# A decoder layer with routed experts: row buffers twice, reciprocals spread by transfers, another order of the sequence stage

## The chip, the cores and the metric

The kernel runs on one core of a Trainium2 chip. The core has five engines with their own instruction queues, each of which works strictly in order: TensorE (PE; its weight loads are shown as PEld), VectorE (DVE), ScalarE (ACT), GpSimd (POOL) and SyncE (SP), which here only issues transfers. They wait for each other through semaphores. The metric is the device time of one execution in microseconds, from the first to the last instruction with what the launch puts around it; the median of several runs counts. The profile and the trace come from one further execution.

## What is computed

A post-norm decoder layer on 16 sequences of 256 tokens, 256 features, all in float32:

```python
# attention 1 (one head): scores q.k, an elementwise function of them, softmax, values, output
theta = BASE_THETA + K_DOP * sigmoid(qk) + K_NOR * tanh(qk) + K_SERO * relu(qk)
attn = softmax(theta, axis=-1)
out = einsum('bst,btd->bsd', attn, v) @ Wo.T + bo
# attention 2 (cross): 16 heads of 16 features, in blocks of 64 tokens, keys and values from ctx
scores = einsum('bnqhd,bnkhd->bnhqk', qh, kh) / sqrt(hd)
out = einsum('bnhqk,bnkhd->bnqhd', softmax(scores), vh) @ out_proj_w.T + out_proj_b
# feed-forward: 32 experts of width 128, 4 chosen per token within 2 of 4 groups, and a shared one
x = layernorm(x + attn1(x)); x = layernorm(x + attn2(x, ctx)); x = layernorm(x + ffn(x))
```

## The kernel before

**Stages.** After a short setup (products of the weights of attention 1, constants), the sequence stage takes the 16 sequences through both attentions, the shared expert and the routing. It scatters each token's row to the four experts chosen, into the DRAM tensor `routed`. Then 159 expert blocks of 128 rows gather from `routed`, and an output stage adds up and normalises.

**The sequence stage is a pipeline written by hand.** On each engine a loop `for t in range(nseq + 5)` names its steps in a fixed order; a step `f(e, t - k)` works for the sequence that is k steps behind. So in step t the engines work on several sequences at once: attention 1 on sequence t, cross attention on t - 1, gates, router and shared expert on t - 3, the shared output and the scatters on t - 4. Nothing else sets the order: each engine does its list from top to bottom, and a wait of one entry holds all that stands behind it. PE starts its step t with `pe_scores2(t - 1)` (L410). The names used below, in PE's order: cross scores `pe_scores2` L410, `pe_x2T` (transposes, L274, as all transposes), `pe_z` L314, `pe_vo` L326, scores 1 `pe_scores1` L335, `pe_shared_out` L541, `pe_router` L507, `pe_gate` L518, `pe_pTa` (transposes of `sha`), `pe_k` L371, `pe_prT` (transposes of the softmax `pr`), `pe_pTb` (of `shb`), `pe_av1` L354, `pe_up` L529, `pe_av2` L464, `pe_den` L447, `pe_v` L381, `pe_rank` L550, `pe_x1T`, `pe_spread` L477, `pe_q` L393, `pe_out2` L487.

**Passes of many small products.** Four passes of PE consist of 32 or 64 products on parts of the array: the cross scores, `pe_av2`, `pe_den` and `pe_spread`. `pe_den` sums the exponentials into one bank (128 rows x 64), DVE's `vec_rden` takes the reciprocals (L1096), and `pe_spread` multiplies them with a 0/1 matrix so that every output dimension has its own reciprocal. ACT copies the product with the values to `num` (`act_num`), and `vec_o` (L1102) multiplies the two:

```python
                            m = e.matmul(bank[7][32 * j:32 * j + 32, at], c("spread")[:, dims:dims + 32], rden[i % 2][:, :],
                                         start=True, stop=True)
```

**Buffers.** The 8 PSUM banks are shared by all passes, which the `after(...)` waits keep apart. `x1`, `kM`, `vM`, `row` and `idx` exist once.

**POOL** adds the constant to the residuals (`pool_xc`, `pool_xc2`), takes the inverse roots of the layer norms (`pool_rs1`, `pool_rs2`), copies each token's row four times into `row` (`pool_row`, L1382) and issues 8 indirect scatters per sequence (L1398, L1405), which wait for the cross scores of the same step. `pool_row` waits until the scatters of the sequence before have landed. DVE's `vec_key` (last operation L1201) gives the rows their places and weights.

**SP** issues in each step `load_xT`, `load_x`, `load_c` (the inputs of the sequence, single buffers), `store_acc`, and `load_rest`, a 768 KB share of the expert weights. `load_rest(0)` first fills a part of `routed` with zeros (`zrow`, 4 MB).

## Time and profile before

| | us |
|---|---|
| median of 3 runs | 878.8 |
| lowest and highest | 878.05, 879.95 |
| the profiled execution | 873.4 |
| its span, first to last instruction | 871.2 |

The profiled execution is 0.6% shorter than the median; the span leaves out 2.2 us around the instructions. The profile has a page of busy times and strips over 40 slices of the span, and the trace behind it answers with timelines of an engine, transfers with their time to landing, and busy times by stretch. Times are microseconds from the start of the span. "L410" is a line of the kernel. The end of a PE row is modelled, so a pass is read from its own start to the start of the next. The count behind a PE row is twice that of the products, since each float32 product is two records.

### The profile page before, as it was taken

How to read it: one execution, taken by the hardware profiler on the slowest of the kernel's cores; microseconds unless marked ns; L12 is line 12 of the kernel's file. 1: busy time of each engine (PE TensorE's matmuls, PEld its weight loads, DVE VectorE, ACT ScalarE, POOL GpSimd, SP SyncE). 2: the span in 40 equal slices, each digit the busy share in tenths (PEclk: the TensorE clock that was granted, in tenths of full speed). 3: DMA queues.
4: the chain of work that ended last, by engine and by line, in shares of the span. 5: the costliest groups of instructions: out<-in, count | busy, mean ns of one | idle time of the engine just before them, and what ended most of it. 6: DMA issues, size and time to landing. Idle time of an engine off the chain costs nothing.

```text
span 871.2 us, 23658 instructions
## 1 busy us (share of the span) xinstructions
PE 801.1 (92%) x7881; PEld 658.8 (76%) x7881; DVE 546.1 (63%) x2115; ACT 461.5 (53%) x1150; POOL 408.3 (47%) x501
## 2 busy tenths in 40 slices
PE   7778999999999999999999555899999999999885
PEld 6567788888888888888887444688888888887332
DVE  2244577887788787887788852355555555554366
ACT  1455566655665666655665111466666666665133
POOL 0200235464455546464545662455656555556123
PEclk9999999999999999999999875999999999999999
DMA  6472223243324322342331124855555555552996
GB/s 222 125 174 79 80 69 103 100 136 93 121 76 142 106 103 82 133 124 94 104 127 58 67 86 134 301 163 166 165 162 159 169 165 158 161 170 91 327 401 242
DMA packets 69654, 125.06 MB, mean 144 GB/s; under 512 B 9665, under 2 KB 43329, under 8 KB 69282
## 3 DMA queue, kind: packets, MB, share of 16 engines
q1 hardware_dynamic: 51394, 81.60, 30.3%
q0 software_dynamic: 13776, 37.77, 12.1%
q10 hardware_dynamic: 4368, 4.20, 1.4%
q8 instruction: 67, 1.10, 0.5%
q14 instruction: 49, 0.40, 0.2%
HBM read 73.16 MB, written 50.36 MB: 142 GB/s over the span
## 4 chain that ended last, share of the span: by engine, by line
PE 78%; DMA 6%; POOL 5%; issue 4%; SPq 4%; ACT 2%; DVE 1%; ACTq 0%; POOLq 0%; DVEq 0%
PE banks L584 15%; PE banks L274 11%; PE banks L597 7%; PE banks L393 4%; SPq L623 4%; PE banks L381 3%; PE banks L354 3%; PE banks L314 3%; PE banks L335 3%; PE banks L371 3%; PE banks L326 3%; PE banks L487 3%; PE banks L518 3%; PE banks L541 3%; PE banks L529 3%
## 5 line engine op out<-in xcount | busy, mean ns | idle before, releaser
L1431 POOL DMA_INDIRECT y<-yb_tile,idcol_tile x159 | 153.0, 962 | 123.6 <-ACT yb_tile L948 121.3
L584 PE MATMUL banks<-w_expert_tile,xbT_tile 128*128 x636 | 166.4, 385 | 3.9 <-ACT xbT_tile L786 3.9
L584 PEld LDWEIGHTS banks<-w_expert_tile,xbT_tile 128*128 128x128 f32 x636 | 109.9, 193 | 13.5 <-issue 4.9
L1259 DVE COPY hbT_tile<-banks 128x128 f32<-128x128 f32 x159 | 46.4, 292 | 117.2 <-PE banks L274 117.2
L1398 POOL DMA_INDIRECT routed<-row_tile,idx_tile x64 | 63.3, 989 | 85.0 <-PE banks L410 66.5
L948 ACT ACTIVATE yb_tile<-banks,rowsb_tile 128x256 f32<-128x256 f32 x159 | 75.4, 474 | 48.8 <-PE banks L597 41.5
L597 PE MATMUL banks<-w_expert_tile,hbT_tile 128*128 x318 | 95.7, 383 | 0.0
L1366 POOL TENSOR_TENSOR rs_tile<-ve_tile,half_neg_tile 128x2 f32<-128x2 f32 x16 | 11.5, 717 | 140.6 <-DVE ve_tile L1046 140.6
L1405 POOL DMA_INDIRECT routed<-row_tile,idx_tile x64 | 65.7, 1027 | 17.7 <-issue 17.7
L942 ACT ACTIVATE gb_tile<-banks 128x128 f32<-128x128 f32 x159 | 44.2, 278 | 55.5 <-PE banks L584 55.5
L786 ACT ACTIVATE xbT_tile<-banks 128x256 f32<-128x256 f32 x159 | 59.9, 377 | 25.5 <-PE banks L274 25.2
L274 PE MATMUL banks<-const_tile,rowsb_tile 128*128 128x128 f32 x318 | 62.0, 278 | 6.9 <-DMA rowsb_tile<-routed 6.9
L274 PEld LDWEIGHTS banks<-const_tile,rowsb_tile 128*128 128x128 f32 x318 | 45.4, 144 | 23.9 <-DMA rowsb_tile<-routed 7.7
L597 PEld LDWEIGHTS banks<-w_expert_tile,hbT_tile 128*128 128x128 f32 x318 | 48.3, 192 | 12.6 <-issue 0.8
L649 PE MATMUL banks<-w_expert_tile,const_tile 128*128 128x512 f32 (+1 forms) x102 | 45.7, 596 | 8.1 <-DMA w_expert_tile<-y 8.1
L1242 DVE SCALAR_TENSOR_TENSOR hb_tile<-gb_tile,banks 128x128 f32<-128x128 f32 x159 | 44.6, 280 | 9.7 <-ACT gb_tile L942 9.6
L1246 DVE TENSOR_TENSOR hb_tile<-hb_tile,banks 128x128 f32<-128x128 f32 x159 | 45.6, 287 | 5.6
L649 PEld LDWEIGHTS banks<-w_expert_tile,const_tile 128*128 128x128 f32 x102 | 19.1, 196 | 35.2 <-DMA w_expert_tile<-y 17.8
L274 PE MATMUL banks<-const_tile,hb_tile 128*128 128x128 f32 x159 | 43.5, 274 | 0.0
L693 ACT ACTIVATE w_expert_tile<-w_expert_tile,fnmr_tile,frs_tile 128x256 f32<-128x256 f32 x32 | 17.6, 593 | 47.2 <-DVE fnmr_tile L673 47.2
L1382 POOL COPY row_tile<-x_tile 128x512 f32<-128x512 f32 x64 | 37.5, 625 | 6.9 <-DMA routed<-row_tile,idx_tile 6.9
L1360 POOL TENSOR_TENSOR xc_tile<-x_sb_tile,c_out_tile 128x256 f32<-128x256 f32 x32 | 23.0, 741 | 31.2 <-DVE c_out_tile L1311 27.4
(205 smaller groups left out, 1847.0 us busy)
## 6 DMA issues: line engine op xcount, KB each, us to landing
rowsb_tile<-routed SPq DMA_DIRECT2D x159, 129.0 KB, 2.2
w_expert_tile<-y SPq DMA_DIRECT2D x15, 1024.0 KB, 16.6
w_expert_tile<-w_expert SPq DMA_DIRECT2D x16, 768.0 KB, 6.3
cT_tile<-ctxT SPq DMA_DIRECT2D x16, 384.0 KB, 3.4
routed<-zrow_tile SPq DMA_DIRECT2D x1, 4128.0 KB, 22.7
xT_tile<-xT SPq DMA_DIRECT2D x16, 256.0 KB, 3.2
x_sb_tile<-x SPq DMA_DIRECT2D x16, 256.0 KB, 3.5
base<-acc_sb_tile SPq DMA_DIRECT2D x16, 256.0 KB, 3.8
```

The source lines that it names most:

```text
L274: return e.transpose(o, i, ident)
L584: m = e.matmul(bank[2 + u % 2][:, 0:2 * EI], xbT[u % 2][:, k * P:(k + 1) * P], w_flat[:, bass.ds(w + k * D, D)], start=k == 0, stop=k == D ...
L597: e.matmul(bank[6 + u % 2][:, 0:D], hbT[u % 2][:, :], w_flat[:, bass.ds(w + 2 * D, D)], start=True, stop=True).then_inc(SEM["p_down"], 1)
L649: m = e.matmul(sum_rows(g), ident, part(g, k), start=k == 0 and g >= 8, stop=k == TOPK - 2)
L786: e.activation(o, i, ACT.Copy).then_inc(SEM[done], 1)
L948: e.activation(yb[n % YS][:, :], bank[6 + u % 2][:, 0:D], ACT.Copy, scale=rowsb[n % ROWS][:, D:D + 1])\
L1242: e.scalar_tensor_tensor(hb1[u % 2][:, :], gb[u % 2][:, :], 1.0, bank[2 + u % 2][:, 0:EI], ALU.add, ALU.mult).then_inc(SEM["v_hb1"], 1)
L1246: e.tensor_tensor(hb[u % 2][:, :], hb1[u % 2][:, :], bank[2 + u % 2][:, EI:2 * EI], ALU.mult)\
L1259: e.tensor_copy(hbT[u % 2][:, :], bank[4 + u % 2][:, 0:EI]).then_inc(SEM["v_hbT"], 1)
L1398: e.indirect_dma_start(routed, bass.IndirectOffsetOnAxis(ap=idx[:, 0, k:k + 1], axis=0), row[:, k, 0, :], None).then_inc(SEM["st_rowa"], 16)
L1405: e.indirect_dma_start(routed, bass.IndirectOffsetOnAxis(ap=idx[:, 1, k:k + 1], axis=0), row[:, k, 1, :], None).then_inc(SEM["st_rowb"], 16)
L1431: e.indirect_dma_start(y, bass.IndirectOffsetOnAxis(ap=idcol[n % ROWS][:, :], axis=0), yb[n % YS][:, :], None).then_inc(SEM[f"st_y{n % YS} ...
```

## The change

1. `pe_spread` and `act_num` are gone. SP stores `rden` to a DRAM tensor `rdd` (`store_den`), and loads it back in two transfers that repeat each row for the 16 dimensions of its head (`load_den`) into `rsp`; `vec_o` reads PSUM and `rsp`.
2. `row`, `idx`, `x1`, `vM`, `kM`, `rs1` and `nmr1` exist twice, one for even and one for odd sequences, with semaphores of their own for the scatters.
3. `pool_row` on POOL becomes `act_row`, one instruction with a repeated source, on ACT.
4. Some tiles of the stage (`t12`, `prT`, `x1T`, the second `kM`) lie in the room of the last two shares of the expert weights, which are therefore loaded in the drain (`LATE` is 2).
5. All passes get other banks, and all engines another order, with `nseq + 6` steps: cross attention is two steps behind, its output three, the second norm four, routing five, shared output and scatters six. POOL's scatters stand behind `pool_rs1` and ahead of `pool_xc`.

```diff
@@ tiles
+        def late(at, n):
+            return w_flat[:, (nseq - LATE) * SHARE + at:(nseq - LATE) * SHARE + at + n]
-        x1 = sa("x1", [P, T, D])
+        x1 = [sa(f"x1{u}", [P, T, D]) for u in range(2)]
-        kM = sa("kM", [P, DK, S // CH, 2, CH])
-        vM = sa("vM", [P, T, NP, VW])
+        kM = [sa("kM0", [P, DK, S // CH, 2, CH]),
+              late(1536, 1024).rearrange("p (k n h c) -> p k n h c", k=DK, n=S // CH, h=2)]
+        vM = [sa(f"vM{u}", [P, T, NP, VW]) for u in range(2)]
-        row = sa("row", [P, TOPK, T, RW])
+        rsp = sa("rsp", [P, DK, S])
+        row = [sa(f"row{u}", [P, TOPK, T, RW]) for u in range(2)]
@@ ACT
+        def act_row(e, i):
+            e.wait_ge(SEM["a_x2"], i + 1)
+            after(e, SEM[f"st_rowa{i % 2}"], 16 * TOPK * (i // 2))
+            after(e, SEM[f"st_rowb{i % 2}"], 16 * TOPK * (i // 2))
+            e.activation(row[i % 2][:, :, :, 0:D],
+                         x2[i % 2][:, :, :].rearrange("p (k t) d -> p k t d", k=1).to_broadcast([P, TOPK, T, D]), ACT.Copy)\
+                .then_inc(SEM["a_row"], 1)
@@ DVE
         def vec_o(e, i, ch):
-            e.wait_ge(SEM["p_spread"], i + 1)
-            e.wait_ge(SEM["a_num"], i + 1)
-            f = num[:, :, :].rearrange("p a b -> p (a b)")
-            e.tensor_tensor(f, bank[7][:, :], f, ALU.mult).then_inc(SEM["v_o"], 1)
+            e.wait_ge(SEM["p_av2"], i + 1)
+            e.wait_ge(SEM["ld_den"], 16 * DK * (i + 1))
+            after(e, SEM["p_out2"], i)
+            e.tensor_tensor(num[:, :, :].rearrange("p a b -> p (a b)"), bank[5][:, :],
+                            rsp[:, :, :].rearrange("p a b -> p (a b)"), ALU.mult).then_inc(SEM["v_o"], 1)
@@ POOL
         def pool_scattera(e, i):
             e.wait_ge(SEM["v_key"], i + 1)
-            after(e, SEM["p_s2"], min(i + 4, nseq))
+            after(e, SEM["p_s2"], min(i + 5, nseq))
@@ SP
+            def store_den(e, i):
+                e.wait_ge(SEM["v_rden"], i + 1)
+                after(e, SEM["ld_den"], 16 * DK * i)
+                e.dma_start(rdd[i % 2].rearrange("r c q -> c r q"), rden[:, :]).then_inc(SEM["st_den"], 16)
+
+            def load_den(e, i):
+                e.wait_ge(SEM["st_den"], 16 * (i + 1))
+                after(e, SEM["v_o"], i)
+                for g in range(DK):
+                    e.dma_start(rsp[:, g, :], rdd[i % 2, g * 8:(g + 1) * 8].rearrange("r c (o q) -> r o (c q)", o=1)
+                                .to_broadcast([8, HD, S])).then_inc(SEM["ld_den"], 16)
...
-                if live(t - 5):
-                    store_acc(e, t - 5)
-                if live(t - 1):
+                if live(t - 6):
+                    store_acc(e, t - 6)
+                if live(t - 2):
+                    store_den(e, t - 2)
+                if live(t - 2):
+                    load_den(e, t - 2)
+                if 0 < t <= nseq - LATE:
                     load_rest(e, t - 1)
+                if nseq < t <= nseq + LATE:
+                    load_rest(e, t - 1 - LATE)
```

**What stands in a row now.** On PE, the end of a middle step and the start of the next (L410), before; L381 are the values, L550 and L551 the rank, L477 the spread pass:

```order
L381 MATMUL banks<-w_cross_tile,cT_tile 128x128 x8
L550 MATMUL banks<-msel_tile,const_tile 128x64
L551 MATMUL banks<-macc_tile,const_tile 128x64
L274 MATMUL banks<-const_tile,x_tile 128x128 x4
L477 MATMUL banks<-rden_tile,const_tile 32x64 x32
L393 MATMUL banks<-x1T_tile,w_cross_tile 128x256 x4
L487 MATMUL banks<-w_cross_tile,num_tile 128x256 x4
L410 MATMUL banks<-kM_tile,qT_tile 64x128 x32
```

The same place on PE in the changed kernel; L546 and L547 are the rank, L403 is `pe_q`, L475 `pe_av2`, L364 `pe_av1`, L392 the values, L421 the cross scores, L324 `pe_z` of the next step:

```order
L546 MATMUL banks<-msel_tile,const_tile 128x64
L547 MATMUL banks<-macc_tile,const_tile 128x64
L403 MATMUL banks<-w_expert_tile,w_cross_tile 128x256 x4
L284 MATMUL banks<-const_tile,pr_tile 128x128 x4
L475 MATMUL banks<-sha_tile,vM_tile 32x64 x16
L475 MATMUL banks<-shb_tile,vM_tile 32x64 x16
L364 MATMUL banks<-vo_tile,w_expert_tile 128x256 x4
L392 MATMUL banks<-w_cross_tile,cT_tile 128x128 x8
L421 MATMUL banks<-kM_tile,qT_tile 64x128 x32
L324 MATMUL banks<-xT_tile,g_qk_tile 128x256 x4
```

The spread pass and the output product (L487) are gone from the step's end, attention 1's product and the values have moved there, and of what stands there only `pe_prT` and `pe_av1` use results of the same step's ACT work.

On SP, one middle step before, from one load of `xT` (L1443) to the next:

```order
L1443 DMA xT_tile<-xT 128x512
L1448 DMA x_sb_tile<-x 128x2x256
L1454 DMA cT_tile<-ctxT 128x768
L1460 DMA base<-acc_sb_tile 128x512
L1472 DMA w_expert_tile<-w_expert 128x1536
L1443 DMA xT_tile<-xT 128x512
```

And on SP in the changed kernel:

```order
L1434 DMA xT_tile<-xT 128x512
L1439 DMA x_sb_tile<-x 128x2x256
L1445 DMA cT_tile<-ctxT 128x768
L1451 DMA base<-acc_sb_tile 128x512
L1457 DMA rdd<-rden_tile 4x32x64
L1463 DMA rsp_tile<-rdd 128x1x256 x2
L1479 DMA w_expert_tile<-w_expert 128x1536
L1434 DMA xT_tile<-xT 128x512
```

The store and the two loads of the reciprocals stand ahead of the weight share and of the next sequence's `xT`, each with its wait.

On DVE in the changed kernel, the end of a step and the first operation of the next, in the middle of the stage; L1098 is `vec_o`, the rows behind it are `vec_x1`, and L1059 is the first maximum over the cross scores:

```order
L1173 TENSOR_TENSOR hs_tile<-hs_tile,banks 128x512
L1098 TENSOR_TENSOR num_tile<-banks,rsp_tile 128x512
L1050 RECIPROCAL den_tile<-den_tile 128x2
L1052 SCALAR_TENSOR_TENSOR xc_tile<-banks,den_tile,xc_tile 128x256 x2
L1036 BN_STATS st_tile<-xc_tile 128x6 x2
L1039 BN_AGGR ag_tile<-st_tile 128x2 x2
L1041 TENSOR_SCALAR neg_tile<-ag_tile 128x2
L1042 TENSOR_SCALAR ve_tile<-ag_tile 128x2
L1059 TENSOR_REDUCE mxa_tile<-banks 128x16
```

Before, `vec_x1` stood in the middle of the step, ahead of the routing's choice, and the step ended with `vec_x2`.

## Rows read from the trace of the kernel before

**Rows 1.** The page of the profile, its parts 1 and 2.
```profile
span 871.2 us, 23658 instructions
PE 801.1 (92%) x7881; PEld 658.8 (76%) x7881; DVE 546.1 (63%) x2115; ACT 461.5 (53%) x1150; POOL 408.3 (47%) x501
...
PEclk9999999999999999999999875999999999999999
```

**Rows 2.** Timeline of PE, one middle step: start us, us, line, tiles, count.
```profile
323.74 1.21 PE L410 MATMUL banks<-kM_tile,qT_tile 32*64 32x128 f32 x64
...
342.61 0.65 PE L464 MATMUL banks<-sha_tile,vM_tile 128*32 128x64 f32 x32
...
347.38 1.10 PE L477 MATMUL banks<-rden_tile,const_tile 128*32 128x64 f32 x64
348.41 1.99 PE L393 MATMUL banks<-x1T_tile,w_cross_tile 128*128 128x256 f32 x8
...
352.06 1.21 PE L410 MATMUL banks<-kM_tile,qT_tile 32*64 32x128 f32 x64
```

**Rows 3.** Timeline of PE, first steps; in brackets idle us before, and its releaser.
```profile
32.12 2.02 PE L381 MATMUL banks<-w_cross_tile,cT_tile 128*128 128x128 f32 x16
36.91 0.66 PE L274 MATMUL banks<-const_tile,x_tile 128*128 128x128 f32 x4 [2.77 <-ACT x_tile L903]
...
79.88 1.97 PE L274 MATMUL banks<-const_tile,sha_tile 128*128 128x128 f32 x8 [2.61 <-ACT sha_tile L875]
```

**Rows 4.** Timeline of PE, start of the drain and of the expert blocks.
```profile
465.51 1.21 PE L410 MATMUL banks<-kM_tile,qT_tile 32*64 32x128 f32 x64
...
534.10 1.35 PE L274 MATMUL banks<-const_tile,rowsb_tile 128*128 128x128 f32 x4 [6.92 <-DMA rowsb_tile<-routed]
```

**Rows 5.** Timeline of DVE, the same middle step.
```profile
330.77 1.22 DVE L1089 TENSOR_TENSOR shb_tile<-banks,mxb_tile 128x1024 f32<-128x1024 f32 x1
...
345.57 0.54 DVE L1096 RECIPROCAL rden_tile<-banks 128x64 f32<-128x64 f32 x1
```

**Rows 6.** Timeline of ACT, the same middle step, copies of 512 and 1,024 columns.
```profile
338.31 0.60 ACT L786 ACTIVATE prT_tile<-banks 128x512 f32<-128x512 f32 x1 [1.80 <-PE banks L274]
338.80 1.02 ACT L884 ACTIVATE sha_tile<-banks 128x1024 f32<-128x1024 f32 x1
```

**Rows 7.** Busy us of each engine in 50 us of middle steps.
```profile
300.00:350.00 50.00, 50.00 (x695) 43.95 (x694) 39.60 (x149) 31.63 (x73) 28.01 (x38) 1.00 0.32 104
```

**Rows 8.** Transfers of the whole run by line: KB each, median us to landing.
```profile
out<-w_expert_tile ACTq DMA_DIRECT2D x2, 128.0 KB, 1.7
```

**Rows 9.** The page, part 6, with the same columns.
```profile
w_expert_tile<-w_expert SPq DMA_DIRECT2D x16, 768.0 KB, 6.3
...
base<-acc_sb_tile SPq DMA_DIRECT2D x16, 256.0 KB, 3.8
```

**Rows 10.** Timeline of SP, one middle step.
```profile
346.69 0.33 SPq L1454 DMA_DIRECT2D cT_tile<-ctxT  x1
...
347.54 0.43 SPq L1472 DMA_DIRECT2D w_expert_tile<-w_expert  x1
```

**Rows 11.** Timeline of POOL, first and last of eight scatters.
```profile
325.75 1.06 POOL L1398 DMA_INDIRECT routed<-row_tile,idx_tile  x1 [4.96 <-PE banks L410]
...
336.38 0.96 POOL L1405 DMA_INDIRECT routed<-row_tile,idx_tile  x1 [0.30 <-issue]
```

**Rows 12.** Timeline of SP, the zero fill and what follows.
```profile
34.64 0.40 SPq L1468 DMA_DIRECT2D routed<-zrow_tile  x1
35.09 12.18 SPq L1472 DMA_DIRECT2D w_expert_tile<-w_expert  x1
49.41 0.33 SPq L1443 DMA_DIRECT2D xT_tile<-xT  x1
```

**Rows 13.** Transfers issued from 48 to 56 us: KB, us to landing.
```profile
xT_tile<-xT SPq DMA_DIRECT2D x1, 256.0 KB, 10.4
```

**Rows 14.** Timeline of DVE, last routing operation of the stage.
```profile
518.82 0.41 DVE L1201 TENSOR_REDUCE row_tile<-mine_tile 128x8 f32<-128x256 f32 x1
```

More of the change, by code:

```diff
@@ L70, in constants @@
     at, out = 0, {}
-    for name, a in zip(("ident", "before", "ones", "headmask", "denmask", "spread", "region", "upto", "blockno", "part", "nowhere"), parts):
+    for name, a in zip(("ident", "before", "ones", "headmask", "denmask", "region", "upto", "blockno", "part", "nowhere"), parts):
         out[name] = (at, a.shape[1])
@@ L158, in build @@
         den = sa("den", [P, T])
-        prT = sa("prT", [P, T, T, P])
+        prT = late(1024, 512).rearrange("p (t u q) -> p t u q", t=T, u=T)
         xc = sa("xc", [P, T, D])
@@ L208, in build @@
         slot = sa("slot", [P, T, 8])
-        idx = sa("idx", [P, T, TOPK], I32)
+        idx = [sa(f"idx{u}", [P, T, TOPK], I32) for u in range(2)]
         ctx_a.close()
@@ L850, in act_prT @@
             after(e, SEM["p_av1"], i)
-            copy(e, prT[:, :, :, :].rearrange("p a b c -> p (a b c)"), bank[7][:, :], "a_prT")
+            copy(e, prT[:, :, :, :].rearrange("p a b c -> p (a b c)"), bank[6][:, :], "a_prT")
         def act_x1T(e, i):
@@ L1284, in _ @@
             e.memset(ev[:, :, :], -BIG)
-            e.memset(vM[:, :, :, :], 0.0)
+            for u in range(2):
+                e.memset(vM[u][:, :, :, :], 0.0)
             ch(e.memset(macc[:, :, :], 0.0))
             e.wait_ge(SEM["g_iota"], 1)
-            ch(e.tensor_copy(row[:, :, :, D + 1].bitcast(I32), dest_id[:, :, :]))
+            for u in range(2):
+                m = e.tensor_scalar(row[u][:, :, :, D + 1].bitcast(I32), dest_id[:, :, :], float(u * T), None, ALU.add)
+            ch(m)
             e.wait_ge(SEM["ld_const"], 16 * 5)
@@ L1375, in pool_rs2 @@
             e.tensor_tensor(nmr2[:, :], neg2[i % 2][:, :], rs2[:, :], ALU.mult).then_inc(SEM["g_rs2"], 1)
-        def pool_row(e, i):
-            e.wait_ge(SEM["a_x2"], i + 1)
-            after(e, SEM["st_rowa"], 16 * TOPK * i)
-            after(e, SEM["st_rowb"], 16 * TOPK * i)
-            for k in range(TOPK):
-                m = e.tensor_copy(row[:, k, :, 0:D], x2[i % 2][:, :, :])
-            m.then_inc(SEM["g_row"], 1)
         def pool_xc2(e, i):
@@ L1489, in _ @@
             e.dma_start(w_shared_out[:, :, :], d["w_shared_out"]).then_inc(SEM["ld_w"], 16)
[L1490 removed]
+            for t in range(nseq + 6):
                 if live(t) and t > 0:
```

499 lines of the change are left out of this document (243 added, 256 removed).

## The prediction

> **What bounds the kernel now.** I read the page first: the engines' busy shares and the strip of TensorE's granted clock [rows 1]. PE is busy 92% of an 871.2 us span, the next engine 63%, and the clock is at its upper level, 2.4 GHz, nearly throughout. The program has three parts: the setup, the sequence stage up to the first expert block at 534.10, and the expert blocks with the output. The change touches the middle part and the setup's bank numbers. Then I read PE's own timeline step by step. A middle step goes from one start of the cross scores (L410) to the next, 323.74 to 352.06, 28.3 us [rows 2]. In it every pass starts where the one before it stops issuing: PE waits for nothing and its work is the bound. Thirteen steps in a row look like this. Before them the ramp has waits (2.77 us for the first layer norm, 2.61 us for an exponential [rows 3]); after them the drain, from 465.51 to 534.10, is 68.6 us long [rows 4], with PE mostly waiting for VectorE and POOL. So an edit in the middle is worth what it takes off PE, while ramp and drain are read by their chains.
>
> **The spread pass goes.** `pe_spread` is 32 products, 347.38 to 348.41, 1.03 us of PE in each of 16 steps [rows 2]; it gives 28.3 - 1.03 = 27.3 us for a full step. This is so only if the new order leaves PE without waits, so I laid one step of it out, with PE's pass widths (differences of starts, as in [rows 2]) from cross scores at 0: z from 1.1, scores 1 from 7.7, the transposes of `shb` from 11.3, `pe_den` 17.1 to 18.1, prT at 22.2, values 25.3 to 27.3. What each waits for is ready earlier: the exponential of `shb` at about 8 (the DVE operation before it ends some 5.8 us in, four operations of 1.2 us each [rows 5]); the copies of `pTa` and `pTb` at about 14; prT's softmax at about 19.5, behind the new `act_row` on ACT, for which I take 1.9 us from the 512- and 1024-element copies (0.60 and 1.02 us [rows 6]). DVE's 39.6 us of 50 are 22.4 us a step, ACT's 31.6 are 17.9, and with the row copy 19.2 [rows 7]: both fit into 27.3. The closest is again prT to its product, 0.1 us, as now. The sum here: 27.3.
>
> **Reciprocals by transfer.** In place of the pass, SP stores `rden` to DRAM, waits for it and loads it back twice with a broadcast. `vec_o` needs it for a product that PE reads only 5.9 us into the next step: hidden by about 9 us of other passes; if that cover went, `vec_o` would hold `vec_x1` behind it on DVE. The dearer thing is SP's queue. Now `load_xT` of the next sequence is issued as soon as scores 1 are done. In the changed order it stands behind the wait for `v_rden`, the store's round trip, two loads of 128 KB and the 768 KB share of expert weights, and `pe_z` of the next step needs it 1.1 us in. No row has this; call L the time from the end of `vec_rden` to the landing of `xT`. Store: between the 1.7 us of 128 KB to `out` [rows 8] and the 3.8 us of 256 KB to `base` [rows 9]; I take 2.3, nearer the small one, as this is 32 KB. Then 1,280 KB in line: the nearest are the 1,408 KB of `cT`, `base` and weights, issued from 346.69 and landed 6.3 us after 347.54, 7.15 us in all [rows 9, 10]; I take 6.9. L = 9.2, bounds 8.2 and 10.95. In a full step the reciprocal (0.54 us [rows 5]) ends at 18.8 and z is due at 28.4, so L may be 9.6: 0.4 us to spare, and every microsecond beyond that is a microsecond in each of about 13 steps.
>
> The Trainium skill speaks against this edit (DMA: Bandwidth & Descriptors, Rules for kernel authors, use all 16 engines): an outermost dimension below 16 confines a transfer to that many engines; here it is 4 for the store and 8 for each load. By it the loads would weigh on half of the engines what twice their bytes weigh on all, and L would tend to the upper bound; no row of before has such a transfer, so I leave the sum as it is; by the rule, rivals 1 and 2 below are what the change would come to.
>
> **Row buffers.** `pool_row` (four copies, 2.3 us of POOL a step) becomes one ACT instruction, and scatters of one sequence need not have landed before the next rows are written. In full steps neither was on PE's path: nothing. In the drain it matters, below. `vM`, `kM`, `x1` twice: they remove waits of PE for ACT and allow attention to be a step further apart. `num` straight from PSUM: 0.6 us of ACT, nothing on the path.
>
> **Scatters.** POOL's eight go now from 325.75 to about 337.3 [rows 11], between the cross scores' end and the av2 pass at 342.61 [rows 2], so they already touch none of the passes of small products; by my layout they go from 1.6 to 12, before `pe_den`. Price nothing; the bound on either side is 0.1 us a step, since the passes run back to back with and without scatters.
>
> **Ramp.** Step 0 ends at 34.0 as now [rows 3]. Step 1 no longer waits for the layer norm; its passes are 13.5 us and its chain (scores, tanh, softmax, transpose, product) makes it 16: next cross scores at 50.1, not 70.7. But z of sequence 2 needs its `xT`, which SP can't issue until 47.3 because the 4 MB zero fill fills the queue (12.18 us on one issue [rows 12]), and which lands about 59.8, as now (49.41 + 10.4 [rows 12, 13]), since the fill is in front of it. So PE stalls 51.2 to 59.8, where before nothing needed that load. After it the step's reciprocal ends about 72.8, so z of 3 at 82.0. From z to the end of `pe_den` are 12.1 us of passes in these steps, 0.6 to the reciprocal, 9.2 of L: 21.9 a step against 20.1 of work. z of 4 at 103.9, of 5 at 125.8, of 6 at 151.2 (25.4 us, routing joins), and ten full steps: z of step 16 would be at 424, its cross scores at 422.9. For the clock at its lower level, 1.2 GHz, after the stalls (a weight of two or three passes at double width) I add 2.5 us: 425.4 against 465.5 now [rows 4].
>
> **Drain.** There are now six steps after the last full one in place of five, and more is left to do. By DVE's operations, from the step's start: 18.9 to the next cross scores (which wait for `vec_key`), 39.6 at the end of the next step's DVE work, 54.3, 65.7, and the last `vec_key` at 76.3. From `vec_key`'s end to the first expert block is 534.10 - 519.2 = 14.9 us [rows 4, 14]: eight scatters and their landing, unchanged. With 1.5 us for the clock 92.7 in all, against 68.6. First block at 425.4 + 92.7 = 518.1, so 534.1 - 518.1 = 16.0 us are gained. The two last weight shares move into the drain, where nothing waits for them for 60 us. After the first block nothing changes.
>
> **Sum.** The profiled execution took 873.4 us, 0.6% below the median 878.8; the gain is a difference of places in it, and I take it from the median: 878.8 - 16.0 = 862.8, rounded 863.
>
> **Rivals.** (1) The next `xT` comes late in every step: L between 9.9 and 10.9. For it: the store's upper bound; against it: the row of 7.15 carries more bytes. It costs 0.3 to 1.3 us in 13 steps and up to 1.7 in the ramp's three: 868 to 877. (2) The same chain beyond L = 10.9, its upper bound: then a full step is over 28.6 us, longer than now, and the time is 880 to 884; slower. It needs the small store to take as long as 256 KB do. (3) The scatters' new place does what the name says and the small passes gain: excluded nearly, as they are clear now. (4) Shorter than laid out: no low clock in ramp and drain (4 us), L at 8.2 (3 us): 853 to 858.
>
> **How the numbers follow.** Forecast, 858 to 868: 0.50. Rival 1: 0.22, of which 0.06 within 0.2% of 878.8, about what a measurement can tell from no change (877.0 to 880.6). Rival 2: 0.12. Rivals 3 and 4: 0.16. Faster by over 0.2%: 0.50 + 0.16 + 0.16 = 0.82; same 0.06; slower 0.12. The range takes in most of rival 4 and rival 1 and leaves out rival 2: 853 to 876.
>
> **What would show it.** Starts of the cross scores 27.3 us apart from step 6 on, without PE idle time put down to `xT`; a PE wait of 8 to 9 us near 51 us for `xT`; the cross scores of step 16 near 425; the first block near 518. If the steps are 28 or more, look at the wait before z: a DMA as its releaser proves rival 1 or 2. A wait before another pass (the transposes of `shb`, prT's product) would mean that my layout of DVE and ACT is wrong. If the steps are 27.3 and the time is not, the drain is what I got wrong.

## The result, and the profile after

The changed kernel takes 909.5 us (median of 4 runs, 906.8 to 911.4) against 878.4 for the kernel before: a ratio of 1.035, 95% interval 1.032 to 1.039. The prediction was 863, with 853 to 876 as its range: wrong in sign, and about 47 us off. The profiled execution has a span of 909.6 us. Line numbers below are the changed kernel's: L421 cross scores, L324 z, L345 scores 1, L382 keys, L457 `pe_den`, L475 attention values, L829 tanh of the scores on ACT, L504 the router's product and L917 ACT's copy of it, L1114 the first operation of DVE's routing, L1391 and L1398 scatters, L1457 the store of the reciprocals, L1463 their loads, L1479 weights, L1434 `xT`.

The page of the changed kernel answers to [rows 1]:
```profile
span 909.6 us, 21550 instructions
...
PE 805.4 (89%) x6857; PEld 655.9 (72%) x6857; DVE 550.7 (61%) x2117; ACT 474.8 (52%) x1150; POOL 369.6 (41%) x437
...
PEclk9979999999999999999988885889999999999998
```
PE has 1,024 records (512 products) fewer and is no less busy, and its idle time grew by 34 us. One middle step, PE's timeline as in [rows 2] (in brackets idle us before, and its releaser; "remote" is a semaphore update for which the profile finds no instruction that ended just then):
```profile
395.53 1.21 PE L421 MATMUL banks<-kM_tile,qT_tile 32*64 32x128 f32 x64
397.84 1.99 PE L324 MATMUL banks<-xT_tile,g_qk_tile 128*128 128x256 f32 x8 [1.10 <-DMA xT_tile<-xT]
...
404.47 1.89 PE L345 MATMUL banks<-xT_tile,zT_tile 128*128 128x256 f32 x8
...
409.69 1.89 PE L382 MATMUL banks<-cT_tile,w_cross_tile 128*128 128x256 f32 x8
412.29 0.63 PE L284 MATMUL banks<-const_tile,x_tile 128*128 128x128 f32 x4 [0.70 <-ACT shb_tile L883]
413.26 1.97 PE L516 MATMUL banks<-x2T_tile,w_shared_in_tile 128*128 128x256 f32 x8 [0.35 <-issue]
...
425.46 1.21 PE L421 MATMUL banks<-w_expert_tile,qT_tile 32*64 32x128 f32 x64
```
The step is 29.9 us, not 27.3 (the others 29.6 to 32.1), and PE waits in two places. Before z it waits for `xT`: 1.2 us here. Before and after the transposes of x1 it waits for ACT's copy of `shb`; from the keys (L382) to the shared gate product (L516) 3.57 us go by, where a step without that wait needs 2.17.

**The first wait** is the chain that the prediction called L. DVE ends the reciprocal at 417.07; then SP's timeline:
```profile
417.10 0.57 SPq L1457 DMA_DIRECT2D rdd<-rden_tile  x1
419.18 1.22 SPq L1463 DMA_DIRECT2D rsp_tile<-rdd  x2
420.45 0.45 SPq L1479 DMA_DIRECT2D w_expert_tile<-w_expert  x1
421.00 0.36 SPq L1434 DMA_DIRECT2D xT_tile<-xT  x1
```
`xT` landed at 427.94 and z started 10.9 us after the reciprocal. Over the 13 steps this is 9.2 to 12.1 us, median 10.5. Before the change SP issued `xT` in mid-step:
```profile
330.76 0.33 SPq L1443 DMA_DIRECT2D xT_tile<-xT  x1
```
It landed 4.6 us later, and z of that sequence started at 353.69: 18 us in hand.

**The second wait** is none of the prediction's. ACT, POOL and PE in the same step:
```profile
404.87 0.65 ACT L820 ACTIVATE vo_tile<-banks 128x256 f32<-128x256 f32 x2
409.66 0.47 ACT L829 ACTIVATE w_expert_tile<-banks,r_half_tile 128x256 f32<-128x256 f32 x1 [4.14 <-remote]
```
```profile
398.13 1.04 POOL L1391 DMA_INDIRECT routed<-row_tile,idx_tile  x1 [0.53 <-issue]
...
407.07 0.96 POOL L1398 DMA_INDIRECT routed<-row_tile,idx_tile  x1 [0.31 <-issue]
```
The tanh needs scores 1, whose products end at 406.4 by PE's rows (404.47 plus 1.89), and DVE's bias, which is there since 402.7. It starts at 409.66, 1.6 us after the last scatter. In nine of ten steps it starts 1.5 to 1.6 us after the last scatter has ended. An instruction tells the others of its completion by a semaphore update, and the trace has a record of the updates. It says why: the completion of scores 1 is on record at 409.63, that of the shared product behind it at 409.73, of the transposes at 409.82 and 409.91. In the full steps completions of PE come up to 4.9 us late and those of DVE up to 1.6 us, many of them in a burst when the scatters are over; of ACT's, which an expectation below names too, none is on record late (a part of them has no record). Before the scatters, and in the ramp's steps that have none, all completions but one are on record 0.01 us after their instruction's end.

The routing beside the scatters is not needed for it. In the step of the same trace that starts at 333.4, ACT's copy of the router's product, which all of the routing waits for, is itself late:
```profile
342.64 0.97 PE L504 MATMUL banks<-w_router_tile,x2T_tile 128*128 128x32 f32 x8
344.65 0.96 POOL L1398 DMA_INDIRECT routed<-row_tile,idx_tile  x1 [0.30 <-issue]
345.60 0.22 ACT L917 ACTIVATE sc_tile<-banks 128x64 f32<-128x64 f32 x1 [2.20 <-remote]
345.86 0.61 DVE L1114 TENSOR_SCALAR sc_tile<-sc_tile 128x64 f32<-128x64 f32 x1 [2.40 <-issue]
```
The product ended at 343.61 and its completion is on record at 345.58, 2.0 us late, before the first operation of the routing. And in the expert blocks, which have no routing and one scatter each, 60 completions of PE are on record up to 1.6 us late.

The one trace of the kernel before has no late completion, in the sequence stage or in its 159 expert blocks. That does not tell how the kernel before fares on the chip of the result: every trace with late completions in the stage, seven in all, has them in the expert blocks too, which the change left as they were, and the traced execution (873.4 us) was 5 us shorter than the median. So it was probably not under the condition in which the result was measured.

The stages, with the first transposes of the expert blocks as the end of the drain:
```profile
566.39 0.69 PE L284 MATMUL banks<-const_tile,rowsb_tile 128*128 128x128 f32 x2 [2.60 <-DMA rowsb_tile<-routed]
```
Cross scores of step 16, the step behind the last full one, start at 455.1 (forecast 425.4; before 465.5), the first block at 566.4 (forecast 518.1; before 534.1 [rows 4]), and from there to the end it is 343.2 us against 337.1 before.

### The profile page after: what moved, and what is told of

Same layout as the page of the kernel before. It is cut to its first block, busy times and chain, and to the rows that moved or that the text cites. A ratio compares the mean times of both kernels' runs of the same rounds, so it can differ in the third digit from the quotient of the medians.

```text
span 909.6 us, 21550 instructions
## 1 busy us (share of the span) xinstructions
PE 805.4 (89%) x6857; PEld 655.9 (72%) x6857; DVE 550.7 (61%) x2117; ACT 474.8 (52%) x1150; POOL 369.6 (41%) x437
## 4 chain that ended last, share of the span: by engine, by line
PE 48%; DMA 16%; DVE 10%; issue 9%; SPq 7%; ACT 4%; another core or an unknown queue 3%; POOL 3%; ACTq 0%; DVEq 0%; POOLq 0%
PE banks L580 14%; DMA xT_tile<-xT 8%; PE banks L284 8%; PE banks L593 7%; SPq L619 3%; PE banks L324 3%; DMA rdd<-rden_tile 3%; PE banks L516 2%; PE banks L335 2%; DMA w_expert_tile<-y 2%; SPq L1479 2%; DMA y<-yb_tile,idcol_tile 2%; PE banks L457 1%; SPq L1463 1%
## 5 line engine op out<-in xcount | busy, mean ns | idle before, releaser
L1384 POOL TENSOR_TENSOR xc_tile<-x_tile,c_out_tile 128x256 f32<-128x256 f32 x32 | 24.8, 797 | 139.3 <-issue 139.3
L1391 POOL DMA_INDIRECT routed<-row_tile,idx_tile x64 | 62.8, 981 | 39.5 <-issue 21.3
L1398 POOL DMA_INDIRECT routed<-row_tile,idx_tile x64 | 61.6, 963 | 19.5 <-issue 19.5
L324 PE MATMUL banks<-xT_tile,g_qk_tile 128*128 128x256 f32 x128 | 39.2, 460 | 29.7 <-DMA xT_tile<-xT 29.7
L324 PEld LDWEIGHTS banks<-xT_tile,g_qk_tile 128*128 128x128 f32 x128 | 27.6, 226 | 37.1 <-DMA xT_tile<-xT 32.8
```

Source lines behind the costliest of these rows:

```text
L324: m = e.matmul(bank[0][:, db * S:(db + 1) * S], g_qk[:, k, db * P:(db + 1) * P], xT[:, k, :], start=k == 0, stop=k == DK - 1)
L1391: e.indirect_dma_start(routed, bass.IndirectOffsetOnAxis(ap=idx[i % 2][:, 0, k:k + 1], axis=0), row[i % 2][:, k, 0, :], None).then_inc(SEM ...
L1398: e.indirect_dma_start(routed, bass.IndirectOffsetOnAxis(ap=idx[i % 2][:, 1, k:k + 1], axis=0), row[i % 2][:, k, 1, :], None).then_inc(SEM ...
```

## The experiments

The kernels of one series ran side by side on one chip, each series on another (the recorded expectations say "call"), and each ratio is to the kernel before on that chip. A ratio is formed from means, without the profiled executions, and can differ by some tenths of a per cent from that of the medians. "Step" is the distance of the cross scores in the middle; "L" is from the end of the reciprocal to the start of z in full steps, and "landed" the time to the landing of `xT` where z does not wait for it.

| series, kernel | median us | ratio (95%) | step us | L us |
|---|---|---|---|---|
| 1 before | 871.6 | | | |
| 1 `e1_xt_first` | 847.8 | 0.974 (0.970 to 0.978) | 27.3 | no wait |
| 1 `e2_scatters_late` | 886.2 | 1.016 (1.011 to 1.020) | 29.1 | 11.4 |
| 1 `e3_both` | 859.5 | 0.985 (0.981 to 0.989) | 27.3 | no wait |
| 1 `e4_weights_behind` | 845.1 | 0.972 (0.965 to 0.979) | 27.3 | no wait, landed 7.4 |
| 2 before | 877.8 | | | |
| 2 `r_after` | 909.5 | 1.034 (1.027 to 1.041) | 29.6 | 10.5 |
| 2 `e5_fill_later` | 904.6 | 1.033 (1.026 to 1.041) | 29.7 | 10.6 |
| 2 `e6_xt_first_fill_later` | 893.9 | 1.018 (1.011 to 1.024) | 29.6 | no wait |
| 2 `e7_no_round_trip` | 897.0 | 1.024 (1.017 to 1.031) | 29.6 | no wait, landed 5.0 |
| 3 before | 868.7 | | | |
| 3 `q_after` | 872.4 | 1.003 (0.999 to 1.006) | 28.3 | 10.7 |
| 3 `q_xt_first` | 847.3 | 0.975 (0.971 to 0.980) | 27.3 | no wait |
| 3 `q_xt_first_scatters_late` | 857.0 | 0.986 (0.982 to 0.990) | 27.3 | no wait |
| 3 `q_xt_first_scatters_split` | 848.3 | 0.976 (0.972 to 0.980) | 27.3 | no wait |
| 4 before | 881.8 | | | |
| 4 `s_fill_later` | 900.7 | 1.018 (1.011 to 1.025) | 29.7 | no wait |
| 4 `s_fill_later_split` | 870.7 | 0.989 (0.985 to 0.992) | 27.8 | no wait |
| 5 before | 870.1 | | | |
| 5 `s_after_scatters_late` | 884.9 | 1.017 (1.012 to 1.021) | 29.0 | 11.4 |
| 5 `s_fill_later_late` | 854.0 | 0.983 (0.978 to 0.987) | 27.3 | no wait |
| 5 `s_fill_later_split_choice` | 847.6 | 0.976 (0.972 to 0.980) | 27.3 | no wait |
| 6 before | 870.3 | | | |
| 6 `u_split_choice` | 849.7 | 0.975 (0.971 to 0.978) | 27.3 | no wait |

**Series 1.** `e1_xt_first`, on SP:
```
+                if live(t + 1) and t > 0:
+                    load_xT(e, t + 1)
                 if live(t - 6):
                     store_acc(e, t - 6)
                 if live(t - 2):
                     store_den(e, t - 2)
```
(and the old place of `load_xT` is gone, `load_xT(e, 1)` stands ahead of the loop).

> The changed kernel with one edit on SP: the load of the next xT is issued as soon as scores 1 are done, ahead of the store of the reciprocals, their two loads and the weights' share. In the changed kernel the time from the end of the reciprocal to the start of the next z is 9.2 to 12.1 us and the full steps are 29.6 to 32.1 us. Theory A (two causes: xT stands behind the round trip and the weights; and completions of PE, ACT and DVE are seen late while POOL scatters during the routing, which costs about 1.3 us before the x1 transposes): PE no longer waits before z, full steps become 28.4 to 28.8 us, the 8 to 10 us wait for the second xT behind the zero fill goes, 880 to 892 us. Rival B (what is late is the broadcast of the reciprocals itself, the wait only moves to the product that reads num): steps stay at 29.5 us or more, above 900 us.

`e2_scatters_late`, on POOL: both scatter functions stand behind `pool_xc`, and the first half has
```
-            after(e, SEM["p_s2"], min(i + 5, nseq))
+            after(e, SEM["v_route"], min(i + 2, nseq))
```


> The changed kernel with one edit on POOL: the eight scatters wait for the end of the routing's selection of the next sequence instead of its cross scores, so that they no longer run beside it (they run from about 14 to 24 us into a step). In the changed kernel the tanh on ACT starts 1.5 us after the last scatter, 3 us after its scores are done. Theory A (scatters beside the routing make semaphores late): tanh starts with its scores, the time from z to the end of the reciprocal falls from 19.3 to about 17.8 us, full steps from 30 to 28.5, 888 to 898 us in all. Rival C (the lateness has another cause, the order of ACT or the DMA traffic of x and cT): tanh stays 3 us late and the time within 4 us of 909.5. Rival D (scatters cost the passes of small products that they now run beside): those passes (reciprocal sums 1.0 us, attention values 1.0 us) grow by a measurable amount each.

> Both edits: xT issued ahead of the round trip, and the scatters after the routing. Theory A: no wait of PE is left in a full step, 27.3 to 27.6 us a step as laid out in the prediction, 866 to 877 us in all. If a third cause is hidden in the full steps, they stay at 28 us or more and the time is above 880.

`e4_weights_behind`: `load_rest(e, t - 2)` directly behind `load_xT(e, t)`, in place of `load_rest(e, t - 1)` at the step's end.

> The changed kernel with one edit on SP: only the weights' share (and the zero fill) moves behind xT; the store of the reciprocals and their two loads stay ahead of it. It tells the two parts of the wait for xT apart. If the 768 KB in line and their issue are the larger part (theory A1), xT lands 6.5 to 7.5 us after the reciprocal, z does not wait in full steps, and the time is that of the kernel with xT first, 880 to 892 us. If the round trip and the two narrow loads are it (theory A2: an outermost dimension of 4 and 8), xT still lands 9 us or more after the reciprocal, steps stay above 29 us and the time above 898.

One edit on SP turns the loss into a gain: 0.974, full steps of 27.3 us. Rival B is out. But theory A had said 880 to 892 for `e1` and `e4` and 866 to 877 for `e3`, and 848, 845 and 860 came: in none of the four traces is a completion in a full step over 0.25 us late, with the scatters where they were. So `e2` could not test what it was made for (its 886 lies near its forecast by another way: the scatters now run beside the round trip, L is 11.4 us, and the drain is 105.1 us long, from cross scores of step 16 at 450.8 to the first expert product at 555.9, against 93.8 for `e1`). `e4` takes L apart, below. With the weights behind it `xT` is in time (landed 6.6 to 8.9 us after the reciprocal), theory A1.

**Series 2**, to see whether the late completions belong to the order or to the chip.

> The changed kernel as it is, once more. In its first trace completions of PE, ACT and DVE instructions were seen up to 3.3 us late while POOL scattered beside the routing, and 5 us were lost in lone expert blocks; in the kernels with one edit on SP alone (xT first, weights behind) nothing of this is left though the scatters stand where they stood, and they are 61 us faster than the changed kernel was, where I had worked out 18 to 30. If the lateness belongs to the program's order (theory A), it shows here again, a full step is 29.6 us or more and the ratio to the kernel before is 1.030 to 1.040. If it belongs to that one chip (theory F), the ratio here is 1.00 to 1.02, with steps of 28.3 to 28.8 us that only the wait for xT explains.

`e5_fill_later`, on SP in step 2 (the fill is taken out of `load_rest`):
```
                     load_c(e, t)
+                if t == 2:
+                    fill(e)
```


> The changed kernel with the 4 MB zero fill issued after the loads of sequence 2 instead of ahead of them; nothing else moved. It prices the ramp's wait alone. In the changed kernel z of sequence 2 starts at 56.0 (after its scores' step began at 45.8), with xT loaded first at 46.9. Expected: z of sequence 2 about 9 us earlier, the later steps as long as in the changed kernel, 7 to 10 us less than the changed kernel beside it. If the fill then delays the loads of the reciprocals or the third xT, it is 0 to 6 us less.

> xT first, and the zero fill after the loads of sequence 2. With xT first alone PE waits 6.0 us at 54.7 for cT of sequence 2, which is behind the fill, and that step takes 27.2 us where the next two take 20.3. Expected: this wait goes, 5 to 7 us less than xT first alone (847.8), so about 842; if the fill now delays the xT of sequence 3, the gain is under 2 us.

`e7_no_round_trip` leaves work out: the reciprocals of sequence 0 scale all others.
```
-                if live(t - 2):
-                    store_den(e, t - 2)
-                if live(t - 2):
-                    load_den(e, t - 2)
+                if t == 2:
+                    store_den(e, 0)
+                    load_den(e, 0)
+                if 2 < t < nseq + 2:
+                    e.wait_ge(SEM["v_rden"], t - 1)
```
(`vec_rden` and `vec_o` then wait for that one store and load only.)

> The changed kernel without the round trip: only the reciprocals of sequence 0 are stored and loaded, every sequence is scaled by them (so the attention's scale is wrong for the others); SP still waits for each reciprocal before it issues the weights and xT. It prices the store and the two narrow loads: in the changed kernel xT lands 9 to 12 us after the reciprocal, with the weights behind it 6.6 to 8.9. Theory A: without the round trip it lands 5 to 6 us after, z does not wait in full steps (27.3 us), 855 to 870 us. If the round trip is not what counts, steps stay above 29 us.

All four have late completions in every full step, and `r_after` repeats the first result. `e6` and `e7` show them alone, since z waits for nothing there: 29.6 us a step, as long as with the wait for `xT`. So on such a chip the two waits do not add up: from the cross scores of step 6 to those of step 16, ten full steps, it is 299.9 us in `r_after`, 299.9 in `e6` and 296.3 in `e7`. What `e6` gains on `r_after` (1.018 against 1.034) it gains in the ramp, 16 us. In `e7`:
```profile
384.64 1.21 PE L421 MATMUL banks<-kM_tile,qT_tile 32*64 32x128 f32 x64
385.77 1.99 PE L324 MATMUL banks<-xT_tile,g_qk_tile 128*128 128x256 f32 x8
...
401.04 0.63 PE L284 MATMUL banks<-const_tile,x_tile 128*128 128x128 f32 x4 [1.39 <-ACT shb_tile L883]
...
414.21 1.21 PE L421 MATMUL banks<-w_expert_tile,qT_tile 32*64 32x128 f32 x64
```
z starts 1.13 us after the cross scores, and the 2.3 us over 27.3 are all at the x1 transposes. My expectation of 855 to 870 missed, because it took the wait for `xT` as the step's only cause; that of about 842 for `e6` (893.9 came) was counted from a chip without late completions. `e5` did what it says in the ramp (z of sequence 2 at 48.3 instead of 60.0) and its cross scores of step 16 come 13.8 us earlier than in `r_after` (444.0 against 457.8), yet its runs spread from 896.8 to 912.5 and overlap those of `r_after` (904.3 to 913.8): the ratios do not tell the two apart.

**Series 3**, the changed kernel beside `xT` first.

> The changed kernel as it is, beside the next three on the same chip. So far the late completions were in both traces of the changed kernel and in all four kernels of the second call, in none of the four of the first call (another chip). Theory F (some chips show it, whatever the order on SP): it is here either in this kernel and in xT first, or in neither. Theory A (the order on SP decides): it is here in this kernel and not in xT first. If it is absent here, the wait for xT alone is left: a step of 28.0 to 28.8 us and a ratio to the kernel before of about 1.01 to 1.02.

> xT first, beside the changed kernel itself. Theory A: full steps of 27.3 us and a ratio to the kernel before of about 0.974, as in the first call. Theory F on a chip with late completions: full steps of 29.5 us with no wait before z, ratio 1.015 to 1.025.

> xT first, and the eight scatters after the routing's selection. If scatters beside the routing are what makes completions late, there are none here on any chip, full steps are 27.3 us and the ratio is about 0.985 (as in the first call, where the scatters' later place made the drain 8 us longer). If the completions are late here too, the routing has nothing to do with it and the steps are 29 us or more.

The split leaves the first half on `p_s2` ahead of `pool_xc`, and gives the second half, behind it, `v_route`.

> xT first, with the four scatters of the first half where they are (1.2 to 6.5 us into a step, before the routing begins at 7.5) and the four of the second half after the routing's selection. If only scatters beside the routing count, completions are not late, full steps are 27.3 us, and the drain is shorter than with all eight late: ratio 0.972 to 0.982. If four scatters in a row anywhere are enough, it shows here too.

Theory A is out and theory F is left: on this chip even the changed kernel has no late completion in a full step, and is at 1.003 (expected for this case: 1.01 to 1.02). Whether it is the chip itself or what went on around it at that time, one series to a chip cannot tell. `q_after` shows the prediction's own step without the second cause:
```profile
span 866.7 us, 21550 instructions
...
PE 784.4 (91%) x6857; PEld 647.8 (75%) x6857; DVE 553.0 (64%) x2117; ACT 476.5 (55%) x1150; POOL 366.9 (42%) x437
```
PE, ACT and POOL of `q_after`, one step:
```profile
267.65 1.21 PE L421 MATMUL banks<-kM_tile,qT_tile 32*64 32x128 f32 x64
269.38 2.00 PE L324 MATMUL banks<-xT_tile,g_qk_tile 128*128 128x256 f32 x8 [0.52 <-DMA xT_tile<-xT]
...
276.01 1.89 PE L345 MATMUL banks<-xT_tile,zT_tile 128*128 128x256 f32 x8
```
```profile
277.94 0.47 ACT L829 ACTIVATE w_expert_tile<-banks,r_half_tile 128x256 f32<-128x256 f32 x1 [0.88 <-PE banks L345]
```
```profile
278.90 0.96 POOL L1398 DMA_INDIRECT routed<-row_tile,idx_tile  x1 [0.30 <-issue]
```
Same program, same scatters, same routing beside them: the tanh starts with the end of its scores, while the last scatter is still to come. From z to the reciprocal it is 17.54 us, then L. The ten full steps are 282.3 us here, and 272.7 in `q_xt_first`.

**The price of the scatters beside small products**, rival 3, is read in `q_xt_first_scatters_late`, POOL and PE of one step:
```profile
262.82 1.04 POOL L1391 DMA_INDIRECT routed<-row_tile,idx_tile  x1 [4.62 <-DVE er_tile L1143]
...
271.74 0.96 POOL L1398 DMA_INDIRECT routed<-row_tile,idx_tile  x1 [0.30 <-ACT x_tile L909]
```
They run from 12.1 to 22.0 us into the step and so over `pe_den`, 17.0 to 18.0. From its start to that of the pass behind it are 1.03 us with the scatters over it (median of `e3_both`) and 1.03 without (`e1_xt_first`). What the later place costs is in the drain: `e3` reaches its first expert product 102.1 us after the cross scores of step 16, `e1` 93.8.

**Series 4**, a chip with late completions again, asks whether the scatters' place causes them.

> xT first, and the zero fill after the loads of sequence 2, once more (before: ratio 1.018 on a chip whose traces show late completions in every full step, 29.6 us a step). On a chip without late completions the ramp's 6 us wait for cT goes: ratio 0.966 to 0.972, full steps 27.3 us. On a chip with them: 1.015 to 1.02.

> The same with the scatters split: four before the routing begins, four after its selection. On a chip with late completions: if they come from scatters beside the routing, full steps fall from 29.6 to 27.3 us and the ratio to 0.970 to 0.985; if the scatters' place beside the routing is not the cause, it stays at 1.01 to 1.02. On a chip without them: within 0.5% of the kernel with the scatters together.

ACT, then DVE, of `s_fill_later`:
```profile
278.88 0.47 ACT L829 ACTIVATE w_expert_tile<-banks,r_half_tile 128x256 f32<-128x256 f32 x1 [5.10 <-remote]
```
```profile
275.18 0.17 DVE L1129 TENSOR_SCALAR gsel_tile<-gr_tile 128x8 f32<-128x8 f32 x1 [1.44 <-DVE gr_tile L1127]
```
and of `s_fill_later_split`:
```profile
288.93 0.47 ACT L829 ACTIVATE w_expert_tile<-banks,r_half_tile 128x256 f32<-128x256 f32 x1 [0.87 <-PE banks L345]
```
```profile
288.83 0.17 DVE L1129 TENSOR_SCALAR gsel_tile<-gr_tile 128x8 f32<-128x8 f32 x1
```
Moving four of the eight off the routing takes the tanh's wait from 5.1 to 0.9 us (what is left of it is the scores themselves, as on the good chip), DVE's wait for its own completion from 1.4 to 0, the step from 29.7 to 27.8 us, and the ratio from 1.018 to 0.989. So on such a chip the place of the scatters does cause the longer step. Whether it is the routing that must stand beside them, or only that eight scatters in a row run while scores 1 and the passes behind it complete, this edit does not separate, and the step at 333.4 above speaks against the routing. What remains in the step, 0.6 us, lies in `pe_den`, which starts as the last scatter ends (1.6 us to the next pass instead of 1.03); completions of the passes before it are up to 1.1 us late. Outside the full steps less is cured: the drain is 101.4 us (107.4 in `s_fill_later`, 91.2 in `q_xt_first_scatters_split`), the part behind the first block 347.4 (345.9 and 337.3), with 84 late completions of PE.

**Series 5 and 6** asked for that rest, but on both chips no completion in a full step came more than 0.41 us late.

> The changed kernel with its eight scatters after the routing's selection and nothing else moved: only the wait for xT is left. From the reciprocal to the landing of xT 10 to 11.5 us on every chip so far, from z to the reciprocal 17.5 us without late completions: full steps of 28.3 us or more, ratio 1.012 to 1.020. If completions are still late (a chip that shows them, scatters beside the choice and the keys), steps are 28.8 to 29.3 and the ratio 1.02 to 1.03, against 1.034 with the scatters beside the routing.

> xT first, fill later, all eight scatters after the selection (14 to 24 us into a step). On a chip with late completions: eight scatters now run beside the choice (17 to 19) and the keys (23 to 26), both shorter rows of small DVE operations than the routing; steps between 27.3 and 28.2 us, ratio 0.985 to 0.995. Without late completions 27.3 us and 0.975 to 0.985, the drain being longer than with the scatters split.

> xT first, fill later, four scatters before the routing, four after the choice (they end before the keys begin), so that no scatter stands beside a row of small DVE operations in a full step. If those rows are what it takes, completions are on time on any chip and full steps are 27.3 us: ratio 0.965 to 0.98. If they are late all the same, steps are 27.8 us as with the second half ahead of the choice.

> The kernel with xT first, the fill later and the scatters four before the routing and four after the choice, once more, in case the chip is one that shows late completions (three of the six calls so far ran on chips whose kernel before takes 870 us and showed none; the others took 878 to 882 and did). On such a chip: full steps of 27.3 us instead of 27.8, ratio 0.975 to 0.987 against 0.9885 with the second half beside the choice. On another chip: 0.976 as in the last call.

`s_after_scatters_late` repeats `e2`: L grows to 11.4 us with the scatters beside the round trip. What the later fill saves is not settled: step 16 comes at 409.0 in `s_fill_later_split_choice`, but at 414.6 in `u_split_choice`, the same kernel on another chip, and at 414.2 in `q_xt_first_scatters_split`, with the fill in its old place. The ratios of the three are 0.975 to 0.976. Whether scatters off the choice as well would bring 27.3 us on a chip with late completions was not seen.

## Why the prediction was wrong

**The spread pass goes, 27.3 us a step: right.** Every kernel in which z does not wait and completions are on time has 27.25 to 27.3 us (median of its full steps), `act_row` takes 1.91 (taken: 1.9), and no pass waits. One such step of `q_xt_first`:
```profile
277.77 1.21 PE L421 MATMUL banks<-w_expert_tile,qT_tile 32*64 32x128 f32 x64
278.90 1.99 PE L324 MATMUL banks<-xT_tile,g_qk_tile 128*128 128x256 f32 x8
...
290.73 1.89 PE L382 MATMUL banks<-cT_tile,w_cross_tile 128*128 128x256 f32 x8
292.46 0.60 PE L284 MATMUL banks<-const_tile,x_tile 128*128 128x128 f32 x4
...
305.02 1.21 PE L421 MATMUL banks<-kM_tile,qT_tile 32*64 32x128 f32 x64
```

**L = 9.2: the term that was mis-sized.** It measured 10.7 in `q_after`, over the threshold of 9.6, and the step became 17.54 + 10.7 = 28.2 (measured 28.3): in kind what rival 1 said. Its price was too low: 868 to 877 is 0.988 to 0.998 of 878.8, and 1.003 was measured; 1.3 us in 13 steps on 862.8 are already 879.7. The store's 2.3 was right: 2.1. The 6.9 behind it was 8.6. I had scaled 7.15 us of 1,408 KB [rows 9, 10] by bytes, and two things are not in bytes. SP's timeline of `e4_weights_behind` and of `e7_no_round_trip`, whose reciprocals end at 377.47 and 376.06:
```profile
377.50 0.57 SPq L1457 DMA_DIRECT2D rdd<-rden_tile  x1
379.58 1.22 SPq L1463 DMA_DIRECT2D rsp_tile<-rdd  x2
380.90 0.40 SPq L1434 DMA_DIRECT2D xT_tile<-xT  x1
```
```profile
376.09 0.33 SPq L1479 DMA_DIRECT2D w_expert_tile<-w_expert  x1
376.52 0.46 SPq L1434 DMA_DIRECT2D xT_tile<-xT  x1
```
`xT` landed at 384.86 and at 380.94. From its issue to its landing, medians of full steps: 2.8 us with nothing in front (`q_xt_first`), 3.9 behind the two loads (`e4`), 4.5 behind the weights (`e7`), 6.7 behind both (`q_after`). The three series were on three chips; with nothing in front it is 2.5 to 2.8 on five chips. So 256 KB of loads add 2.2 us (6.7 - 4.5) where 768 KB of weights add 2.8 (6.7 - 3.9), and their issue holds SP for 1.22 us on top: 3.4 us for a fifth of the bytes, where 6.9 scaled by bytes has 1.4.

The rule that the prediction set beside the sum (the Trainium skill, DMA: Bandwidth & Descriptors, Rules for kernel authors) agrees with the trace in the number of engines, if one landing record stands for one engine, and in L near its upper bound of 10.95, but not in the way there. The trace has 16 landing records for each transfer of `xT` and of weights, 8 for each load with 8 as its outermost dimension and 4 for the store with 4. But the loads do not hold back half of the engines: in the step of `q_after` whose `xT` was issued at 375.94, 14 of its 16 records come 4.0 to 4.6 us after the issue, about as in `e7` without the loads, and the last two at 6.5 and 6.9. Both loads had landed by 377.55. What holds these two back is not shown.

**"Scatters: price nothing": the step that failed.** I laid the scatters against PE's passes of small products and stopped there. The same table of orders had moved DVE's routing, from 11.8 us into a step (335.52 in the trace of before) to 7.6, so that it stands beside the last four of the eight scatters and no longer beside the last two. In three of the seven comparisons (the first result among them) completions come late while the scatters run, and at this place that costs 2.3 us in each full step (27.3 to 29.6), more in the drain, where the routing is on the critical chain, and, as an estimate, 3 to 9 us behind the first block (341.0 to 347.4 against a median of 338.5 in the other traces). For the ten full steps up to step 16 the forecast was 273 us; they are 272.7 with `xT` first and completions on time, 282.3 with L alone, 296.3 and 299.9 with late completions alone (`e7`, `e6`), 299.9 with both (`r_after`). So on the chip of the result the price of nothing for the scatters is the error of the full steps, and L adds next to nothing to it there. That scatters beside small products cost nothing was itself right where completions are on time.

**Ramp.** The stall for `xT` of sequence 2 is there:
```profile
45.75 1.21 PE L421 MATMUL banks<-kM_tile,qT_tile 32*64 32x128 f32 x64
...
55.98 2.50 PE L324 MATMUL banks<-xT_tile,g_qk_tile 128*128 128x256 f32 x5 [9.03 <-DMA xT_tile<-xT]
```
9.0 us, taken 8.6. The steps behind it are 25.5 and 24.7 us and not 21.9: L is 9.2 to 11.0, and from z to the reciprocal it is up to 14.4 us where `q_xt_first`, without a stall there, has 12.75 (granted clock from 75 to 126 us: 0.93 in this trace, 1.00 in `q_xt_first`). With the 2.5 us for the lower clock the ramp was still forecast about 3 us too short, by both terms.

**Drain: right without the second cause.** In `q_after` it is 92.3 us (436.5 to 528.8), forecast 92.7. In the changed kernel's first trace it is 111.3. Behind the first block `q_after` needs 337.9 us, before 337.1; the first trace 343.2, with the late completions of the expert blocks. "After the first block nothing changes" is right for the program and not for the chip: traces with late completions have 341.0 to 347.4 us there, the others 334.8 to 339.7.

**Sum.** `q_after` has step 16 at 436.5 where 425.4 was forecast: 3 us from the ramp, 8 from L in full steps. That alone takes the forecast gain of 16 us down to 5 in the trace, and to nothing in the timed runs (1.003). The changed kernel's first trace adds 19 us by step 16, 19 in the drain and 5 in the expert blocks. By places, then, the first trace is 54 us longer than forecast (30 by step 16, 19 in the drain, 6 behind the first block); the medians are only 47 apart, since the trace of before was 5 us shorter than its median and this one 2 us longer. L is rival 1's mechanism and explains the first 10 us or so where completions are on time; the rest no rival had. The time lies beyond rival 2's 880 to 884 too, but L stayed below its 10.9 in most steps.

## What to carry to other kernels

A load that the next step needs early must not be queued behind a round trip of the present step: the same changed kernel with `load_xT` one place up is 2.5% faster than the kernel before, on chips where as it stood it gained nothing. On a chip with late completions it was still slower than the kernel before (1.018, with the zero fill later), until half of the scatters had moved as well (0.989). Where an order is changed by a table, lay each moved piece against everything that every engine does there, not against the passes that the change's name speaks of. Small broadcast loads are not priced by their bytes alone: their number, their shape and their issue count. And a trace may come from another condition than the median that it is used with: compare a part that the change does not touch, here the expert blocks, before a difference of places is taken from it.

## What the hardware showed that I had not expected

While POOL issued eight scatters back to back, semaphore updates of PE came up to 5 us late and those of DVE up to 2.2 us, many in a burst 1.5 us after the last scatter. Of the seven comparisons three showed it (kernel before: 877.8 to 881.8 us) and four did not (868.7 to 871.6 us), those of series 1 to 6 each on another chip; for the same program it was 1.034 there and 1.003 here. On these chips completions of PE are late in the expert blocks too, up to 2.5 us, with one scatter in each block. The kernel before was never traced on such a chip; that it takes about 9 us more there would fit late completions in its expert blocks, but is not shown. Four scatters fewer at that place took all but 0.6 us off the full step and 6 us off the drain, and nothing off the expert blocks.

What in the chips differs stays open, and so does what besides the scatters it needs: small DVE operations stood beside them in most steps, but the router's product was late before any of these had begun. A kernel without any scatters was not run, nor one without the routing.
